# Attention and mixture-of-experts block on one core: a new order of five engines, and a split output projection for two of four batches

## The reference

```python
q, k, v = split_heads(xn @ Wq), split_heads(xn @ Wk), split_heads(xn @ Wv)   # 16 heads of 64
q, k = apply_rope(q), apply_rope(k)
sim = where(causal, q @ k.T * 64**-0.5, -inf)
attn_out = (softmax(sim) @ v) @ Wo + bo
logits = xn @ gate_w.T + gate_b                 # 32 experts
probs = softmax(logits, over the tokens)        # each expert takes its 8 best tokens
merged = sum over those 8 tokens of value * xn
o = [gelu([merged, 1] @ w1), 1] @ w2            # w1 (32, 257, 1024), w2 (32, 1025, 256)
ffn_out = o scattered back to the 8 tokens, times the values
out = x + attn_out + ffn_out
```

## Time and profile before

| | |
|---|---|
| median of 3 runs | 1472.28 us (1469.73 to 1473.02) |
| the profiled execution | 1472.21 us |
| its span, first to last instruction | 1470.3 us |
| mean granted clock of TensorE | 0.979 of full |
| busy: PE, POOL, DVE, ACT | 1366.1, 961.0, 865.1, 615.3 us |
| DMA | 188.71 MB, 128 GB/s over the span |

### The profile page before, as it was taken

One profiled execution on the slowest core, in us unless ns is written; L12 is line 12 of the kernel. 1 busy time (PEld: TensorE's weight loads), 2 busy tenths in 40 slices (PEclk: granted clock), 3 DMA queues, 4 the chain that ended last, 5 costly groups with the idle time before them and its releaser, 6 DMA issues.

```text
span 1470.3 us, 30876 instructions
## 1 busy us (share of the span) xinstructions
PE 1366.1 (93%) x11412; PEld 887.6 (60%) x11412; DVE 865.1 (59%) x1169; ACT 615.3 (42%) x937; POOL 961.0 (65%) x662
## 2 busy tenths in 40 slices
PE   5789989888799899899999999999999999999989
PEld 4456656555455555555775666666666776666647
DVE  5976665555456565555436645676666446666731
ACT  4366554434234433442234323445444324454430
POOL 3566666655366556666557756878878668888861
PEclk9899999999899999999999999999999999999999
DMA  5323334655865775565343222122232221212111
GB/s 169 110 80 131 130 130 161 230 203 189 285 206 184 264 259 187 197 219 163 108 138 102 77 78 68 59 77 70 94 103 84 67 74 63 89 59 74 45 48 59
DMA packets 122670, 188.71 MB, mean 128 GB/s; under 512 B 29664, under 2 KB 57728, under 8 KB 122528
## 3 DMA queue, kind: packets, MB, share of 16 engines
q1 hardware_dynamic: 96096, 119.19, 25.1%
q10 hardware_dynamic: 26384, 67.41, 13.4%
q0 software_dynamic: 48, 0.13, 0.1%
HBM read 130.58 MB, written 22.54 MB: 104 GB/s over the span
## 4 chain that ended last, share of the span: by engine, by line
PE 73%; DVE 10%; DMA 8%; issue 4%; ACT 3%; SPq 1%; POOL 0%; ACTq 0%; POOLq 0%; DVEq 0%
PE t_pO L1312 14%; PE t_pF L1287 11%; PE t_pA L1210 8%; PE t_pB L1210 6%; DMA t_swap<-t_raw 5%; PE t_pF L1270 5%; PE t_pC L1363 4%; PE t_pB L1363 4%; PE t_pA L1234 3%; PE t_pC L1234 2%; PE t_pA L1215 2%; PE t_pC L1321 2%; DVE t_LO L966 2%; PE t_pB L1215 2%; DVE t_OT L934 1%
## 5 line engine op out<-in xcount | busy, mean ns | idle before, releaser
L675 POOL TENSOR_TENSOR t_acc<-t_acc,t_PT 128x1024 f32<-128x1024 f32 (+3 forms) x256 | 434.3, 1697 | 177.7 <-ACT t_PT L746 157.9
L650 POOL TENSOR_TENSOR t_swap<-t_swap,t_sin 128x512 f32<-128x512 f32 x124 | 162.2, 1308 | 238.2 <-DMA t_swap<-t_raw 237.8
L1312 PE MATMUL t_pO<-t_PT,t_V 128*64 128x512 f32 (+3 forms) x1536 | 290.9, 500 | 7.3 <-ACT t_PT L746 4.5
L746 ACT ACTIVATE t_PT<-t_pA 128x1024 f32<-128x1024 f32 x192 | 169.5, 883 | 305.9 <-PE t_pA L1222 265.5
L1287 PE MATMUL t_pF<-t_xT,t_wqk 128*128 128x512 f32 x756 | 215.1, 421 | 3.5 <-DVE t_xT L1090 2.7
L966 DVE TENSOR_TENSOR t_LO<-t_rot,t_HI 128x512 fp32r<-128x512 f32 x124 | 157.0, 1266 | 83.6 <-ACT t_HI L778 83.6
L1312 PEld LDWEIGHTS t_pO<-t_PT,t_V 128*64 128x64 f32 x1536 | 93.8, 136 | 144.5 <-issue 121.2
L653 POOL TENSOR_TENSOR t_rot<-t_rot,t_swap 128x512 f32<-128x512 f32 x124 | 174.6, 1408 | 9.7
L1287 PEld LDWEIGHTS t_pF<-t_xT,t_wqk 128*128 128x128 f32 x756 | 135.9, 193 | 45.2 <-issue 12.7
L768 ACT ACTIVATE t_raw<-t_pF 128x512 f32<-128x512 f32 x124 | 74.0, 597 | 187.6 <-PE t_pF L1287 138.6
L942 DVE TENSOR_REDUCE t_nm<-t_pC 128x2 f32<-128x256 f32 (+2 forms) x96 | 71.5, 773 | 135.8 <-PE t_pC L1240 135.8
(11 more groups left out here) (189 smaller groups left out, 2347.7 us busy)
## 6 DMA issues: line engine op xcount, KB each, us to landing
t_w1t<-in_L_ffn_w ACTq DMA_DIRECT2D x32, 1024.0 KB, 6.6
t_w2t<-in_L_ffn_w ACTq DMA_DIRECT2D x32, 1024.0 KB, 9.8
t_swap<-t_raw SPq DMA_DIRECT2D x248, 128.0 KB, 2.1
t_OT<-r_s SPq DMA_DIRECT2D x128, 128.0 KB, 3.0
t_wqk<-wqk_s SPq DMA_DIRECT2D x24, 512.0 KB, 4.1
xt_s<-t_xs SPq DMA_DIRECT2D x6, 1024.0 KB, 4.9
t_xT<-xt_s SPq DMA_DIRECT2D x6, 1024.0 KB, 7.4
t_wvs<-wv_s SPq DMA_DIRECT2D x12, 512.0 KB, 3.8
```

The source lines that it names most:

```text
L650: pool.tensor_tensor(swap_of(r), swap_of(r), sin[:, c * BANK:(c + 1) * BANK], ALU.mult).then_inc(sin_sem, 1)
L675: pool.tensor_tensor(a[:, :, off:], a[:, :, off:], pt, ALU.add).then_inc(acc_done, 1)
L746: act.activation(PT[:, n % PTS, :, 0:w], bank[:, :, 0:w], ACT.Exp, scale=SCALE).then_inc(exp_done, 1)
L1312: mm = pe.matmul(pO[h * DH:(h + 1) * DH, off:], v, PT[:, n % PTS, h, 0:w], start=(j == 0), stop=(j == 4 * c + 3))
```

## The change

Constants of the order:

```diff
-MOE = 5
+MOE = 6
@@ maxima_of
+    if (P, g) == (-1, 3):
+        return pair, [[(3, 0, 512)]]
+    if (P, g) == (-1, 4):
+        return pair, [[(4, 0, 512)], [(4, 512, 128), (5, 512, 256)], [(5, 0, 512)]]
@@ chunks_of
-    return CHUNKS[2 * g:2 * g + 2] if 0 <= P < N else []
+    if P < 0:
+        P, g = 0, g - 4
+    elif P == 0 and g < 2:
+        return []
+    return [(P, c, j) for c, j in CHUNKS[2 * g:2 * g + 2]] if P < N else []
@@ outputs_of
-        tiles = {0: [(0,), (1,), (2,), (3,), (4,), (5,)], 1: [(6,), (7,), (), (), (), ()]}.get(p, [()] * GROUPS)[g]
+        tiles = {0: [(), (0,), (1,), (2,), (3,), (4,)], 1: [(5,), (6,), (7,), (), (), ()]}.get(p, [()] * GROUPS)[g]
@@
-STATISTICS_AT = {(0, 0): 1, (0, 1): 2, (0, 2): 3}
-MOMENTS_AT = {(0, 4): 1, (0, 5): 2, (1, 0): 3}
+STATISTICS_AT = {(0, 1): (2, 0), (0, 3): (2, 1), (0, 4): (3, 0), (0, 5): (3, 1)}
+MOMENTS_AT = {(1, 1): 1, (1, 4): 2, (2, 1): 3}
-FIRST_FILLS = [("k", 0, 0), ("q", 0, 0), ("v", 0, 0), ("v", 0, 2), ("q", 0, 1), ("k", 0, 1)]
+FIRST_FILLS = [("k", 0, 0), ("q", 0, 0), ("v", 0, 0), ("q", 0, 1), ("k", 0, 1), ("v", 0, 2)]
```

SP issues the swap ahead of most else in a stage, and `store_sums` and `spread_recip` are cut in two so that the waits for the way through DRAM stand behind it:

```diff
             for s, (P, g) in enumerate(STAGES):
+                n = normalise_of(*STAGES[s - 1]) if s else None
+                if n is not None:
+                    store_sums(n)
+                n2 = normalise_of(*STAGES[s - 2]) if s >= 2 else None
+                if n2 is not None:
+                    store_recip(n2)
+                f = fill_of(P, g)
+                if f in ROPE:
...
+                        sp.dma_start(swap[o::2, r % 2, :], raw[1 - o::2, :]).then_inc(swapped[r % 2], 16)
+                if n is not None:
+                    load_sums(n)
+                if n2 is not None:
+                    spread_recip(n2)
                 for x_ in slots_of(*STAGES[s - 1]) if s else ():
                     after_slot(*x_)
```

ACT takes Gelu behind the high half and the eviction of its stage, and issues the reads of x (`load_xt`) instead of SP, with the same waits and in the same stages, behind the eviction. DVE makes D (`shift`) ahead of `low` and `combine` at g = 1. Layer2's wait:

```diff
-                    pe.wait_ge(slot_read, n if kind == "layer2" else n - 1)
+                    pe.wait_ge(slot_read, max(n - 1, SLOT["turn", G, k] + 1) if kind == "layer2" else n - 1)
```

The output projection of batches 1 and 2. Wo is split once, the high half on ACT at the end of (15, 3), the low half on DVE at (15, 4), and for batch 3 Wo is loaded again by SP at (25, 3):

```diff
+                if (P, g) == (N - PAIRS + 1, 3):
+                    sp.wait_ge(y_mm, (B - 1) * NT)
+                    sp.dma_start(wot[:, :, :], wo.rearrange("(k p) n -> p k n", p=P128)).then_inc(wo_loaded, 16)
@@ ACT, at the end of the stage ahead of a tile's
+            def round_out(y, t):
+                n = (y - 1) * NT + t
+                act.wait_ge(o_done, 2 * (y * PAIRS + PAIRS - 1) + t // 4 + 1)
+                act.wait_ge(y_mm, max(NT + n - 1, NT))
+                act.activation(oh[:, t % 2, :, :], OT[:, :, t * P128:(t + 1) * P128], ACT.Copy).then_inc(oh_done, 1)
@@ DVE, the same
+            def rest(y, t):
+                n = (y - 1) * NT + t
+                dve.wait_ge(oh_done, n + 1)
+                if n >= 2:
+                    dve.wait_ge(y_mm, NT + n - 1)
+                dve.tensor_tensor(ol[:, t % 2, :, :], OT[:, :, t * P128:(t + 1) * P128], oh[:, t % 2, :, :].bitcast(F32),
+                                  ALU.subtract).then_inc(ol_done, 1)
@@ PE, output
+                if y in (1, 2):
+                    pe.wait_ge(ol_done, (y - 1) * NT + t + 1)
+                    pe.wait_ge(wo_lo, 1)
+                    a = 0
+                    for k in range(PAIRS):
+                        for o, hw in ((oh, 0), (oh, 1), (ol, 0)):
+                            pe.matmul(bank, o[:, t % 2, k, :], woh[:, hw, k, :], start=(a == 0), stop=False)
+                            a += 1
@@ SP, spread_recip, b >= 2
-                    sp.wait_ge(y_mm, (b - 1) * NT + 4 * c + 4)
+                    sp.wait_ge(ol_done, (b - 2) * NT + 4 * c + 4)
```

More of the change, by code:

```diff
@@ L417, in turns_before @@
         def turns_before(s):
-            return sum((g == 1 and 0 <= P < N) + (g == 4 and 0 <= P + 1 < N) for P, g in STAGES[:s])
+            return 1 + sum((g == 1 and 0 <= P < N) + (g == 4 and 0 < P + 1 < N) for P, g in STAGES[:s])
         def swap_ready(engine, r):
@@ L897, in _ @@
                     load_w2(1)
-                if g == 1 and 0 <= P - MOE < E // GE:
-                    act.wait_ge(slot_read, SLOT["layer1", P - MOE, GE - 1] + 1)
-                    act.activation(gh[:, :, :], gh[:, :, :], ACT.Gelu).then_inc(g_done, 1)
                 f = fill_of(*STAGES[s - 2]) if s >= 2 else None
@@ L905, in _ @@
                     evict(fill_of(P, g))
+                if g == 1 and 0 <= P - MOE < E // GE:
+                    act.wait_ge(slot_read, SLOT["layer1", P - MOE, GE - 1] + 1)
+                    act.activation(gh[:, :, :], gh[:, :, :], ACT.Gelu).then_inc(g_done, 1)
+                b = P // PAIRS + 1
+                if P % PAIRS == PAIRS - 2 and 0 < b < B:
+                    if g == 0:
+                        for u in range(2):
+                            act.wait_ge(xs_stored[u], (B - 1) * 16)
+                        act.wait_ge(proj_done, FILL["q", P + 1, 0] + 1)
+                        load_xt(b, 0)
+                    if g == 4:
+                        act.wait_ge(proj_done, FILL["v", P // 2, 6] + 1)
+                        load_xt(b, 1)
                 w = weights_of(P, g)
@@ L1108, in first_maximum @@
                 maximum(0, m, (pC, pA)[m % 2], FIRST_MAXIMA[m])
+            dve.wait_ge(x0_loaded[0], 16)
+            statistics(0, 0)
+            moments(0)
+            dve.wait_ge(stat_done[0], STAT)
+            for t in (2, 3):
+                dve.tensor_scalar(xn[:, 0, t, :], xn[:, 0, t, :], mean[:, 0, t:t + 1], rstd[:, 0, t:t + 1],
+                                  ALU.subtract, ALU.mult).then_inc(xn_done2, 1)
+            dve.wait_ge(x0_loaded[1], 16)
+            statistics(1, 1)
+            first_low(0)
+            weights_low(("qk", 0))
+            weights_low(("v", 0))
+            moments(1)
             dve.wait_ge(g_trans, 1)
@@ L1421, in first_maximum, with warm @@
                 maximum(0, m, (pC, pA)[m % 2], FIRST_MAXIMA[m])
+            def warm(n):
+                for i in range(n):
+                    pe.matmul(pO[:, 0:P128], ident[:, :], ident[:, :], start=True, stop=True)
             pe.wait_ge(ident_made, 2)
+            warm(12)
             pe.wait_ge(g_loaded, 16)
@@ L1427, in _ @@
             tr.then_inc(g_trans, 1)
-            for i in range(12):
-                pe.matmul(pO[:, 0:P128], ident[:, :], ident[:, :], start=True, stop=True)
             first_transposes(0)
+            warm(6)
             fill(("k", 0, 0))
@@ L1491, in _ @@
                         slot(*x_)
-                for c, j in chunks:
-                    values(P, c, j)
+                for chunk in chunks:
+                    values(*chunk)
                 for x_ in slots:
```

197 lines of the change are left out of this document (100 added, 97 removed).

## The result

Over five runs of each the changed kernel takes 1454.9 us (1452.21 to 1461.01) where the one before takes 1472.28 (1469.15 to 1475.09): the ratio is 0.9884, 95% interval 0.9862 to 0.9906. The gain is 17.4 us where 47 were forecast. The profiled execution has a span of 1453.1 us against 1470.3, so the two traces differ by 17.2, and this is what has to be found in them.

The account below looks back on a forecast made before the run. PE, 93% busy, was taken as the bound: PE work, or PE waiting or clocked down. Terms -22 - 2 - 2.5 - 4 - 8 - 4 - 6 + 1 = -47.5 gave 1425 us, range 1404 to 1451.

Parts of the forecast that it names:

- Layer2, -22: Expert pairs: layer2 needs only the turn's read, so all 14 waits for DVE's bias add go, -22 us (-22 to 0).
- Gelu and D, -2: Expert pairs: D made before the low half, Gelu behind the eviction; 0.3 us less idle in 7 pairs, -2 us.
- +16: Upper end for the moved Gelu: exp comes 2.3 us later in 7 pairs if the swap lands no sooner.
- rival A: Weights hold shared DMA engines, swaps land as late as before, Gelu costs +16, reads gain 0: 1449 us, chance 0.17.
- The reads of x, -2.5 and -4: Reads moved to ACT's queue stop delaying swaps: -2.5 us around pair 6, -4 us (0 to -7) at pairs 15 and 23.
- Start and pair 0, -8: Before and in pair 0: earlier first projection, chunks moved ahead, DVE statistics spread; -8 us (0 to -28).
- routing -4: Token choice split over three stages, experts from pair 6: pair 3's stall and clock loss mostly go, -4 us (-7 to 0).
- Outputs, -6 + 1: Output projection: fp32r matmuls save 0.37 us a tile in 16 tiles, -6 us; splitting Wo once costs +1 us.
- B: Rival: half of layer2's 22.0 us returns as second scores waiting, start gives only 3: 1441 us, chance 0.17.

Follow-up runs that it names:

- layer2_old_wait: The changed kernel with layer2's old wait, for the read of the slot just before it: 1464.04 us, ratio 0.9954 to the kernel before.
- gelu_front: The changed kernel with the Gelu back in front of the high half and the eviction of its stage: 1435.64 us, ratio 0.9766 to the kernel before.
- x_reads_on_sync: The changed kernel with the six reads of x issued by SP again instead of ACT: 1449.86 us, ratio 0.9856 to the kernel before.
- three_mended: The changed kernel with the edits of gelu_front and low_before_statistics, and batch 0's first output stores and loads ahead of the swap in 14.0: 1423.51 us.
- x_read_later: The kernel of three_mended with batch 2's read of x issued one stage later, in 14.1 instead of 14.0: 1420.9 us.
- low_before_statistics: The changed kernel with chunk 1's low half of x and q's first turn ahead of batch 1's statistics in DVE's starting list: 1443.03 us.
- output_fp32: The changed kernel with all batches' output projection in fp32, without rounding, split or second load of Wo: 1461.64 us.
- gelu_moved_alone: The kernel before with one edit: the Gelu moved behind the high half and the eviction on ACT: 1489.7 us, ratio 1.0128.
- layer2_alone: The kernel before with one edit, the new wait condition of layer2: 1455.01 us, ratio 0.9891.
- sync_order_before: The changed kernel with SP's whole old order, the reads of x staying on ACT's queue: 1459.26 us, ratio 0.9919.

## Why the prediction was wrong

The forecast of 1425 missed by 30 us, on the side of too much gain; 1454.9 lies outside the range. The direction held, and so did the terms outside the expert pairs and batch 0's outputs, if not always for the reason given. Step by step:

- *Layer2, -22.* Right in mechanism: all 14 waits went. The wait of 3.6 us for an add in 6.0 is not this term's, since layer2_old_wait has it too (3.5); alone in the kernel before, 4.8 did come back behind an add. The size: -16 alone, -9 (median) or -15 (the pairs) in the changed kernel. The step that failed is that all 22.0 were counted as gain.
- *Gelu and D, -2, "ACT does the same work in another order, and exp ends within 0.3 us of where it did".* This is the step that failed most. It rested on the swap coming 3 us sooner. The swap for 8.2 is issued at the same moment, 5.4 us before 8.2 instead of 5.9, since its eviction sets that (SP waits 2.4 us for it before and 6.7 now), not what stands in SP's list around it; what fell is its flight. The DMA issues of that moment, before and after:

```profile
t_swap<-t_raw SPq DMA_DIRECT2D x2, 128.0 KB, 6.7
```

```profile
t_swap<-t_raw SPq DMA_DIRECT2D x2, 128.0 KB, 5.2
```

  So it landed 1.3 us sooner, the Gelu put 2.34 behind it, and exp came 1.0 later, while D, made early, brought PE to the wait sooner. By gelu_front the moved Gelu cost 19 us, near the +16 that the text kept as an end and gave to rival A. The sign of being wrong that the text named was there: ACT's eviction waiting for the swap in front of the Gelu, 1.31 us in 8.2. What D gave by itself no run parts. The half clock behind such a wait was in the term for the reads and in routing, and not in this one.
- *The reads of x, -2.5 and -4.* The other queue brought nothing: x_reads_on_sync loses nothing without it, and no fill waited for x. Of the -4.8 measured at pairs 15 and 23, only 1 to 2 us are clear of scatter, so that the -4 came true by luck. In 14.0 and 14.1 of three_mended the first O on SP's queue took 7.3 us to land, with the read of x in flight from ACT's queue for 4.8 of them, and the second, with the read gone, 3.9. In x_read_later, where the read was issued 3.0 us after the first O, the two took 5.3 and 7.8. The Trainium skill (DMA: Bandwidth & Descriptors, "Issuing engines are not separate DMA queues") says that DMAs of different issuing engines run on the same engines and interleave. The trace agrees by these four times, and rival A had this part right.
- *Start and pair 0, -8, routing -4.* Measured -9.9 together. The first scores of 0.2 came at 68.0, not four us sooner than the 59.4 of before but 8.7 later, at clock 0.83 and 0.85 where before had 0.86 and 0.93; low_before_statistics puts 7.3 of the 8.7 on two misplaced operations. 0.2 to 0.5 then took 27.6 us instead of 38.1: PE had the same matmuls there, but DVE 25.2 us of work instead of 32.6, and the two waits of 3.3 us each for DVE were gone. So pair 1 began 1.8 us sooner; the other 8 of the 9.9 lie in the pairs up to the experts, where pair 1 alone took 36.1 instead of 43.1. That the sum came out near -12 is in part luck: its way, an earlier 0.2, did not happen. What routing gave by itself no run parts.
- *Outputs, -6 + 1.* Measured -8.2, and -6.7 by the median of output_fp32; the +1 for the split shows as 0.3 in pair 15. The matmul was mis-sized: 0.128 us was read from a fill whose first one takes 0.22. In the tile most take 0.120, and a tile's 24 take 2.88 to 2.96 us, 0.49 to 0.57 less than 3.45 and not 0.37. Copies and rests were hidden, as said.
- *What the sum did not have:* +8.0 at 14.1. Two moves met there. The swap was moved ahead of `after_slot` and `start_output`, and the text did not ask what waits behind the swap's own wait: 4 to 5 us. The experts' shift put the first output on the stage that reads x: some 4 us. Nor did it have the +5.1 in the plain pairs.
- *The rivals.* None describes it whole. A had the Gelu's +16 and the reads' 0 right, but for a swap as late as before, and it landed 1.3 us sooner. That its 1449 lies near 1454.9 is in part luck, since it has neither 14.1 nor the plain pairs nor the smaller gain of layer2. In B the waits of layer2 come back as second scores waiting for the same adds; no wait of that kind is due to the new condition in the changed kernel.

## What to carry to other kernels

When an operation is moved on an in-order engine, write down what each of its neighbours waits for, on both sides of the move: the Gelu filled the time of a wait, and behind that wait it was all on the path; the swap, moved up, took its own wait ahead of stores that PE needed. A moved stage must also be laid over what else happens at its new place. And an idle time is worth more than its length where the clock falls behind it.

## What the runs showed of the hardware

In 8.2 before, PE idled 1.33 and 0.77 us and kept the full clock. After, it idled once for 3.57 us, until 423.18, and then ran at 0.50 of full speed, its 1.2 GHz level:

```profile
423.58:426.99 3.41, 3.41 (x20) 2.96 (x15) 1.92 (x4) 1.27 (x3) 3.33 (x3) 0.50 0.07 17
```

All eight expert pairs had such a stretch at or behind that wait. In gelu_front, with waits of 1.6 to 2.2 us, three of eight did, and in three_mended, with waits of 1.6 to 2.0, six: part of the scatter between these two, 370.9 and 379.6 us for the pairs, is clock.

The trace of before had this price, and the prediction did not put it on the moved Gelu. Behind the 4.34 us that PE waited for an exp in 6.2 (the longest of that row, until 347.80) stands:

```profile
348.39:351.81 3.42, 3.42 (x16) 3.09 (x18) 1.49 (x3) 1.38 (x3) 3.03 (x3) 0.50 0.29 97
```

The waits of 3.3 us in 0.2 and 0.4 and of 3.6 us in 13.1 of that trace have one too, and so has one of 2.16 us for D in 10.2, while those of 2.29 and 2.27 in 9.2 and 12.2 have none. In this trace and in the changed kernel's, every wait of over 3 us from pair 0 on cost clock, and of those around 2 us some did. gelu_moved_alone has one of 3.26 us, in 0.2, that did not.

Six idle times before value products, 4.7 us in all, end at nothing the profile shows ("issue"). Four of them, 4.0 us, stand in plain pairs (19, 22, 26 and 29) and make most of the +5.1 there. They go with SP's new order: in plain pairs the ten traces with that order have one to five each, and the four with the old one, those of before, layer2_alone, gelu_moved_alone and sync_order_before, have none. What PE lacked at these moments is not seen, and the cause stays open.
